# A five-step graph network on one Trainium2 core: where x and the output weights are transposed, and when adjacency pairs load

## The reference

```python
Af = A.astype(float32)                       # 2048 x 2048, symmetric, 0 or 1
state = x                                    # 2048 x 256
for _ in range(5):
    s_in  = state @ in_W.T + in_b
    s_out = state @ out_W.T + out_b
    a = concat([Af @ s_in, Af.T @ s_out, state])
    r = sigmoid(a @ r_W.T + r_b)
    z = sigmoid(a @ z_W.T + z_b)
    h = tanh(concat([Af @ s_in, Af.T @ s_out, r * state]) @ h_W.T + h_b)
    state = (1 - z) * state + z * h
out = tanh(state @ o1_W.T + o1_b) @ o2_W.T + o2_b
return layernorm(x + out)
```

## Time and profile before

| | |
|---|---|
| median of 3 runs | 664.06 us (664.0 to 664.29) |
| profiled execution | 664.53 us |
| its span, first to last instruction | 662.7 us |
| TensorE matmul busy | 650.3 us, 98%, 2940 instructions |
| VectorE busy | 516.4 us, 78% |
| ScalarE busy | 348.5 us, 53% |
| GpSimd busy | 51.9 us, 8% |
| mean granted TensorE clock | 0.995 of full speed |
| DMA | 46.72 MB, 90515 packets, 72176 of them under 512 bytes |

### The profile page before, as it was taken

How to read it: one execution, slowest core, us unless ns; L and a number is a source line. 1 busy time by engine, 2 the same in 40 slices (tenths; PEclk the granted TensorE clock), 3 DMA queues, 4 the chain that set the end, 5 groups by cost and what they waited for, 6 DMA issues and landing times.

```text
span 662.7 us, 8577 instructions
## 1 busy us (share of the span) xinstructions
PE 650.3 (98%) x2940; PEld 539.6 (81%) x2940; DVE 516.4 (78%) x838; ACT 348.5 (53%) x486; POOL 51.9 (8%) x49
## 2 busy tenths in 40 slices
PE   8999999999999999999999999999999999999993
PEld 7888888888888888888888888888888888888883
DVE  4976878699687969967796997687789858855886
ACT  2873735477156337724562683366057525724646
POOL 0074034200500000000000000000000000000002
PEclk9999999999999999999999999999999999999998
DMA  8996533213000130300003022000322200013003
GB/s 293 305 405 242 169 130 107 42 42 54 2 0 32 50 47 33 50 14 0 32 33 62 0 63 32 0 32 32 52 44 60 35 1 1 0 64 127 1 2 130
DMA packets 90515, 46.72 MB, mean 70 GB/s; under 512 B 72176, under 2 KB 78960, under 8 KB 90224
## 3 DMA queue, kind: packets, MB, share of 16 engines
q1 hardware_dynamic: 86128, 45.77, 23.9%
q10 hardware_dynamic: 4352, 0.53, 0.5%
HBM read 32.12 MB, written 11.53 MB: 66 GB/s over the span
## 4 chain that ended last, share of the span: by engine, by line
PE 93%; DVE 2%; SPq 2%; DMA 2%; ACT 1%; issue 0%; DVEq 0%
PE bank L561 26%; PE bank L548 17%; PE bank L550 17%; PE bank L549 17%; PE bank L612 15%; DMA stage<-in_adj_dram 2%; SPq L393 1%; DVE stats L1560 1%; DVE a L1553 0%; DVE ring L1136 0%; SPq L389 0%; ACT a L1120 0%; DVE work L1593 0%; SPq L391 0%; DVE work L1588 0%
## 5 line engine op out<-in xcount | busy, mean ns | idle before, releaser
L561 PE MATMUL bank<-ring,rows 128*128 128x512 f32 x768 | 178.8, 389 | 0.3 <-ACT stateT L1091 0.3
L561 PEld LDWEIGHTS bank<-ring,rows 128*128 128x128 f32 x768 | 144.0, 188 | 30.6 <-ACT stateT L1091 0.5
L901 ACT ACTIVATE work<-work,bias 128x512 f32<-128x512 f32 x120 | 86.2, 723 | 155.5 <-DVE work L1280 154.9
L1280 DVE SCALAR_TENSOR_TENSOR work<-degree,deg_w,bank 128x512 f32<-128x512 uint16 x120 | 88.7, 745 | 57.5 <-PE bank L550 56.5
L548 PE MATMUL bank<-u_c,fold 128*128 128x512 f32 x240 | 93.5, 389 | 0.0
L550 PE MATMUL bank<-u_c,fold 128*128 128x512 f32 x240 | 93.4, 389 | 0.0
L549 PE MATMUL bank<-u_c,fold 128*128 128x512 f32 x240 | 93.4, 389 | 0.0
L612 PE MATMUL bank<-ring,rows 128*128 128x512 f32 x256 | 65.1, 391 | 0.0
L548 PE MATMUL bank<-st_c,own 128*128 128x512 f32 x160 | 62.3, 389 | 0.0
L550 PE MATMUL bank<-st_c,own 128*128 128x512 f32 x160 | 62.2, 389 | 0.0
L549 PE MATMUL bank<-st_c,own 128*128 128x512 f32 x160 | 62.2, 389 | 0.0
(11 more groups left out here) (148 smaller groups left out, 985.0 us busy)
## 6 DMA issues: line engine op xcount, KB each, us to landing
stage<-in_adj_dram SPq DMA_DIRECT2D x15, 512.0 KB, 8.8
sums<-in_adj_dram SPq DMA_DIRECT2D x13, 512.0 KB, 8.5
turned_dram<-work SPq DMA_DIRECT2D x12, 512.0 KB, 2.6
rows<-turned_dram SPq DMA_DIRECT2D x192, 32.0 KB, 2.0
work<-in_x_dram SPq DMA_DIRECT2D x4, 512.0 KB, 10.2
x_dram<-work SPq DMA_DIRECT2D x4, 512.0 KB, 8.9
a<-x_dram SPq DMA_DIRECT2D x4, 512.0 KB, 5.3
a<-in_adj_dram SPq DMA_DIRECT2D x3, 512.0 KB, 11.5
```

The costliest lines, as they stand in the source:

```text
L561: m = nc.tensor.matmul(u_bank[2 * (c % 2) + d][:, :], rows[:, part, j, d * P:(d + 1) * P], tile[:, jj, :], start=(first and jj == 0 and pa ...
L901: nc.scalar.activation(gates[:, g, e, :], gates[:, g, e, :], ACT.Tanh if g == H else ACT.Sigmoid, bias=bias[:, g, e:e + 1]).then_inc(gate_ ...
L1280: nc.vector.scalar_tensor_tensor(out=gates[:, g, e, :], in0=degree[:, c * CW:(c + 1) * CW], scalar=deg_w[:, g, e:e + 1], in1=g_bank[s % 3] ...
```

## The change

- The output weights are no longer transposed on TensorE in the preparation. They are loaded as 32 x 32 squares that already lie in the place of their transpose (16 DMAs in runs of 128 bytes, `o_load`, issued ahead of pair 17). VectorE transposes the squares (`o_turn`), ScalarE and VectorE split them (`o_high`, `o_low`), all in gate chunk 0. `PREP` shrinks to 12 items.
- Chunk 0 of x is still transposed on TensorE, now ahead of the H fold. Chunks 1, 2 and 3 are loaded a second time as squares (8 DMAs each, `x_load`): chunk 1 ahead of pair 18, chunk 2 ahead of pair 26 and after chunk 1's are moved, chunk 3 after the last pair, into staging slot 0. VectorE transposes them straight into `stateT` (`x_turn`) at the places that `MOVED_AT` names.
- SyncE loads chunk k of x ahead of pair 2k, so two adjacency pairs load between the chunks. ScalarE and VectorE split x in the same rhythm.
- The store of the split output weights (`o_dram`) moves from before pair 9 to before pair 24. The first part of the degrees gets a place of its own in `t_flat` and no longer waits for that store.

```diff
@@ -140,7 +140,7 @@
         o_w = t_flat[:, 0:4 * DB * D].rearrange("p (a n k d) -> p a n k d", a=2, n=2, k=DB)
         t_rows = t_flat[:, :].rearrange("p (a n w) -> p a n w", a=2, n=3)
-        deg_part = t_flat[:, 0:CW]
+        deg_part = t_flat[:, 4 * DB * D:4 * DB * D + CW]
         res = sums[:, :, :, :].rearrange("p s k w -> p (s k w)").bitcast(F32).rearrange("p (c w) -> p c w", c=NC - 1)
...
@@ -151,7 +151,8 @@
         early = stateT[:, :, :].rearrange("p d n -> p (d n)")
         gate_raw = [g.rearrange("p (b k) -> p b k", b=DB) for g in (late[:, 0:NR], late[:, NR:2 * NR], res.rearrange("p c w -> p (c w)")[:, 0:NR])]
-        o_raw = late[:, 2 * NR:2 * NR + 2 * DB * D].rearrange("p (n b k) -> p n b k", n=2, b=DB)
+        o_squares = late[:, 2 * NR:2 * NR + 2 * DB * D].rearrange("p (n w) -> p n w", n=2)
+        o_T = late[:, 2 * NR - 2 * DB * D:2 * NR].rearrange("p (n w) -> p n w", n=2)
         gate_T = [g.rearrange("p (m d) -> p m d", d=D) for g in (early[:, 0:2 * DB * D], degree[:, :].bitcast(F32))]
         lin_raw = early[:, 2 * DB * D:4 * DB * D].rearrange("p (n b k) -> p n b k", n=2, b=DB)
...
@@ -183,6 +184,8 @@
+        x_spare = {1: stateT[:, :, 3 * CW:4 * CW], 2: stateT[:, :, 3 * CW:4 * CW], 3: staged[0].bitcast(F32)}
         PACK = 8
...
@@ -309,17 +317,16 @@
         std_ready = sem("f_std_ready")
-        N_PREP = NG * 4 + 2
+        N_PREP = NG * 4
         PREP = [(0, R), (1, R), ("fold", R), (0, Z), (1, Z), ("own", Z), ("own", R), (0, H), (1, H), ("own", H),
-                ("fold", Z), ("o", 0), ("o", 1), ("fold", H)]
-        SPLIT = [item for item in PREP if item[0] in ("own", "fold", "o")]
-        ACT_AHEAD = {("own", H): [("x", 0)], ("o", 1): [("x", 1), ("x", 2)],
-                     ("fold", H): [("turned", 0), ("pair", 0), ("turned", 1), ("pair", 1)]}
-        DVE_AHEAD = {("own", H): [("degree", R)], ("fold", Z): [("degree", Z)],
-                     ("o", 1): [("x", 0), ("degree", H)], ("fold", H): [("x", 1), ("x", 2)]}
+                ("fold", Z), ("fold", H)]
+        SPLIT = [item for item in PREP if item[0] in ("own", "fold")]
+        ACT_AHEAD = {("own", H): [("x", 0)],
+                     ("fold", Z): [("x", 1), ("pair", 0), ("pair", 1)], ("fold", H): [("turned", 0), ("turned", 1)]}
+        DVE_AHEAD = {("own", H): [("x", 0), ("degree", R)], ("fold", Z): [("degree", Z), ("x", 1), ("degree", H)]}
         def times_read(item):
...
@@ -385,25 +392,50 @@
             sp.dma_start(gate_raw[R][:, :, 2 * D:], r_v[:, :, 2 * D:]).then_inc(r_loaded[2], 16)
             sp.dma_start(gate_raw[H], h_W.rearrange("(b p) k -> p b k", p=P)).then_inc(w_loaded[1], 16)
-            for n, w in enumerate((o1_W, o2_W)):
-                sp.dma_start(o_raw[:, n], w.rearrange("(b p) k -> p b k", p=P)).then_inc(o_loaded, 16)
             for n, b in enumerate((in_b, out_b)):
                 sp.dma_start(lin_bb[:, n], b.partition_broadcast(P)).then_inc(io_b_loaded, 16)
-            for c in range(NC):
-                sp.dma_start(x_raw[:, c * BC:(c + 1) * BC, :], x_v[:, c * BC:(c + 1) * BC, :]).then_inc(x_loaded[c], 16)
+            def o_load():
+                for n, w in enumerate((o1_W, o2_W)):
+                    for q in range(NQ):
+                        for k in range(DB):
+                            sp.dma_start(o_squares[q * SQ:(q + 1) * SQ, n, k * D:(k + 1) * D].rearrange("a (i c) -> a i c", c=SQ),
+                                         w[:, k * P + q * SQ:k * P + (q + 1) * SQ].rearrange("(i a) c -> a i c", a=SQ)).then_inc(o_loaded, 16)
+            def x_load(c, spare):
+                for q in range(NQ):
+                    for e in range(DB):
+                        sp.dma_start(spare[q * SQ:(q + 1) * SQ, e, :].rearrange("a (i c) -> a i c", c=SQ),
+                                     x[c * CW:(c + 1) * CW, e * P + q * SQ:e * P + (q + 1) * SQ].rearrange("(i a) c -> a i c", a=SQ))\
+                          .then_inc(x_squares[c], 16)
             for c in range(NC):
                 for p in range(NP):
                     q = c * NP + p
+                    if q < NP and q % 2 == 0:
+                        k = q // 2
+                        sp.dma_start(x_raw[:, k * BC:(k + 1) * BC, :], x_v[:, k * BC:(k + 1) * BC, :]).then_inc(x_loaded[k], 16)
                     if (c, p) == (NC - 1, NP // 2):
                         turn_store(0, 0)
+                    if (c, p) == (2, 1):
+                        o_load()
+                    if (c, p) == (2, 2):
+                        sp.wait_ge(prep_read, times_read(("fold", H)))
+                        x_load(1, x_spare[1])
+                    if (c, p) == (NC - 1, 2):
+                        sp.wait_ge(x_moved, DB)
+                        x_load(2, x_spare[2])
                     slot, loads = slot_of(q)
                     if q == IN_RES:
                         sp.wait_ge(prep_read, times_read(("own", NG - 1)))
                         sp.dma_start(o2_bb, o2_b.partition_broadcast(P)).then_inc(o2_b_loaded, 16)
-                    if q == IN_RES + 2:
-                        sp.wait_ge(prep_read, times_read(("o", 1)))
+                    if (c, p) == (NC - 1, 0):
+                        sp.wait_ge(o_split, 2)
                         sp.dma_start(o_dram, t_flat[:, 0:4 * DB * D].bitcast(F32)).then_inc(o_stored, 16)
                     if 2 * NP <= q < 2 * NP + NC:
...
@@ -422,6 +454,9 @@
                     sp.dma_start(staged[slot], adj_v[:, 2 * p:2 * p + 2, c * CW:(c + 1) * CW]).then_inc(stage_loaded[slot], 16)
+            sp.wait_ge(pair_ready, last_in(0) + 1)
+            sp.wait_ge(pair_stored, last_in(0) + 1)
+            x_load(3, x_spare[3])
             turn_store(0, 1)
             for k in range(2):
...
@@ -508,7 +543,7 @@
             pool.wait_ge(o2_b_loaded, 16)
             pool.wait_ge(x_hi, NC)
-            pool.wait_ge(x_read, NC * DB)
+            pool.wait_ge(x_read, DB)
             pool.wait_ge(x_split, NC)
             for c in range(NC):
...
@@ -567,7 +602,9 @@
                 wait(pe, u_lo, (c - 1) * TWO)
-                pe.wait_ge(x_read, min(NC * DB, (c + 1) * TWO))
+                pe.wait_ge(prep_read, times_read(("own", Z)) if c == 0 else N_PREP)
+                if c == 1:
+                    pe.wait_ge(x_read, DB)
                 for p in range(NP):
                     pe.wait_ge(pair_ready, c * NP + p + 1)
...
@@ -628,7 +665,7 @@
                 if first:
                     if c == 0:
-                        pe.wait_ge(x_read, NC * DB)
+                        pe.wait_ge(prep_read, N_PREP)
                     if c < NC - 1:
                         degrees(c)
...
@@ -686,21 +723,20 @@
             def turn_x():
-                for c in range(NC):
-                    pe.wait_ge(x_loaded[c], 16)
-                    for d in range(DB):
-                        m = c * DB + d
-                        pe.wait_ge(prep_read, times_read(PREP[N_PREP + m - 8]))
-                        for b in range(BC):
-                            last = nc.tensor.transpose(bank[m][:, b * P:(b + 1) * P],
-                                                       x_raw[:, c * BC + b, d * P:(d + 1) * P], ident[:, :])
-                        last.then_inc(x_turned, 1)
+                pe.wait_ge(x_loaded[0], 16)
+                pe.wait_ge(prep_read, times_read((0, H)))
+                for d in range(DB):
+                    for b in range(BC):
+                        last = nc.tensor.transpose(bank[DB + d][:, b * P:(b + 1) * P], x_raw[:, b, d * P:(d + 1) * P], ident[:, :])
+                    last.then_inc(x_turned, 1)
             def prepare():
                 for n, (kind, g) in enumerate(PREP):
                     b_ = prep_bank(n)
+                    if (kind, g) == ("fold", H):
+                        turn_x()
                     if n >= 8:
                         pe.wait_ge(prep_read, times_read(PREP[n - 8]))
...
@@ -863,6 +896,8 @@
                 if not (isinstance(t, int) and t == 0):
                     act.wait_ge(state_new, (t - 1) * S_TWO + c * TWO + e + 1)
+                elif c > 0:
+                    act.wait_ge(x_moved, (c - 1) * DB + e + 1)
                 wait(act, gate_done, t * S_GATE + (c - 1) * GATE + 2 * DB)
                 high(st_c[:, HI, e, :], stateT[:, e, c * CW:(c + 1) * CW], st_hi)
...
@@ -921,6 +956,8 @@
                     if first and (c, s) == (NC - 2, 0):
                         degree_part(NC - 1)
+                    if first and c == 0 and s in (2, 3):
+                        o_high(s - 2)
                     if s < DB:
                         rs_high(t, c, s)
...
@@ -1050,10 +1089,9 @@
                     for p in range(DB, NP):
                         expand_staged(0, p)
-                        turned_x(p)
-                        if p == DB:
-                            x_high(NC - 1)
-                    act.wait_ge(x_read, NC * DB)
+                        if p % 2 == 0 and p < NP - 2:
```

(27 more changed lines are left out.)

27 lines of the change are left out of this document (15 added, 12 removed).

## The result

| | before | after |
|---|---|---|
| median | 664.17 us (664.0 to 664.99) | 678.81 us (677.92 to 680.61) |
| ratio, 95% interval | | 1.0223 (1.0211 to 1.0234) |
| profiled execution, its span | 664.53, 662.7 us | 678.04, 676.2 us |
| mean granted clock | 0.995 | 0.985 |

The change makes the kernel 2.2% slower. 669.8 us was predicted, with 674.0 as the upper end. The direction was right. The loss from before's median, 14.6 us, is more than twice the 5.7 us forecast.

A forecast was written before the change was run, and what follows sets the result against it. TensorE's nearly unbroken stream was taken as the first bound, DMA second, VectorE third. Terms -3.7 + 0.8 + 0.1 + 2.9 + 5.6 = +5.7 us, added to the median 664.06, gave 669.8 us, range 666.0 to 674.0.

The forecast's parts named there:

- Part 1: Start: TensorE loses 32 small matmuls and pair 0 is ready in time, so aggregation starts near 21.7, -3.7 us.
- Part 2: Adjacency pairs between x chunks: pair 7 lands about 34.1, cast by 35.2, wanted at 34.4, +0.8 us (0 to 2).
- Part 3: Gate chunk 0: added VectorE work of about 3.8 us eats slack, +0.1 us (0 to 0.5); full time if VectorE is late.
- Part 4: Chunk 0: 24 loads on SyncE's queue ahead of the last residual store delay VectorE's first product, +2.9 us (0 to 5).
- Part 5: Before gate chunk 3: x chunk 3's eight loads ahead of the row loads delay T2, +5.6 us (4.5 to 7.5).
- rival C: Before chunk 3: as the main forecast, and TensorE's clock falls in the 5.6 us gap; chance 0.20.
- B: Chunk 0: the residual store lands in time and pairs are not delayed, +2.8 us, 666.9 us; chance 0.20.
- D: At T2: row loads barely late, the 5.6 us vanish; without the residual wait too, -2.8 us, 661.3 us; chance 0.09.
- E: x's 128-byte runs drain at half the row loads' pace; Part 4 and Part 5 each grow about 3 us, 676 us; chance 0.06.

The follow-up runs named there:

- e7_x_first: Kernel with both edits (24 loads behind the residual store, x chunk 3 on ScalarE's queue), plus all four x chunks loaded ahead of pair 0: 662.04 us.
- e3_both: Changed kernel with the 24 loads behind the last residual store and x chunk 3's loads on ScalarE's queue: 661.04 us, ratio 0.9958.
- e6_x1_late: Changed kernel with only x chunk 1's eight loads moved behind the last residual store; the output weights' 16 stay ahead of pair 17: 673.12 us.
- e1_late: Changed kernel with the 16 output-weight loads and 8 of x chunk 1 moved behind the last residual store and pair 19: 667.20 us.
- e5_wide: Changed kernel with the same 24 loads at the same places, as whole rows (768 runs, not 8,192), so values not transposed: 673.11 us.
- e8_fill0: Changed kernel with 28 matmuls on constants filling TensorE's first wait of 6.3 us in chunk 0: 679.94 us.
- e4_fill: Changed kernel with 18 matmuls, their result unread, filling TensorE's wait before gate chunk 3 in step 0: 677.21 us.
- e2_x3_on_act: Changed kernel with x chunk 3's eight loads issued on ScalarE's queue at the start of gate chunk 2: 672.87 us.

## Why the prediction was right and wrong

**Part 1 (-3.7) was right.** -3.50 at the first aggregation matmul, -3.70 at the gates of chunk 0. e7_x_first, which loads x ahead of the pairs, gains 2.7 us up to the same gates, and the pairs give 1.2 us more in e3_both. The forecast put the 3.7 down to matmuls and to pair 0 being ready in time, without splitting it.

**Part 2 (+0.8 for pair 7) did not come.** The stream of 128 matmuls has no gap in it, 29.28 us against 29.48. Pair 7 came in time: ScalarE, after a wait of 1.77 us for it, started its cast at 32.99, where the forecast had it land at 34.1, and was done at 34.05, before TensorE wanted it at 21.87 + 7 x 1.81 = 34.5. ScalarE waited 0.24 to 0.28 us for each of the next five pairs.

**Part 3 (+0.1) was right for a kernel without other lateness.** In e3_both VectorE's added work costs nothing. Its other sentence, that it costs its full time if VectorE is late, holds too: from the product to the degree cast VectorE was busy 21.42 of 25.38 us before, and 24.73 of 25.01 after. The idle 3.96 us in which it could have caught up are filled. 10.03 us late at the product, less 0.37, gives the 9.66 us. It also says why half clock costs nothing in after's profile: VectorE ran almost without a gap, and the clock was back (1.00 from 72 us) before the matmuls that do not wait for it (from 72.99). In the five other profiles with a late product it was 0.50 during part of them, for 1.6 to 2.8 us lost. No part of the forecast has a fall of the clock in chunk 0.

**Part 4 (+2.9) had the right mechanism and is the mis-sized term: with part 3 it measured +9.7.** The store was to land at 60.8 and landed at 67.0. Two terms of that step, the issue time of the loads and the landing time of the store, failed.
- *The issue: 56.2 predicted, 59.62 measured.* I took 0.50 us a load from the earlier trace rows, where little else moves. Here the 24 loads took 17.5 us rather than 12. Within the 16 loads of the weights the time of one differs:

```profile
44.45 3.59 SPq L403 DMA_DIRECT2D a<-in_L_gnn_o_W_dram  x3
```

```profile
47.59 3.90 SPq L403 DMA_DIRECT2D a<-in_L_gnn_o_W_dram  x8
```

```profile
39.50:48.00 8.50, 8.50 (x39) 7.06 (x38) 7.85 (x14) 6.55 (x9) 7.19 (x6) 1.00 0.97 278
48.00:51.50 3.50, 3.50 (x17) 2.88 (x17) 0.09 (x1) 0.00 (x0) 3.34 (x3) 1.00 0.45 69
```

  The first excerpt is of 45 to 48 us, three loads in 3.59 us; over the first eight (39.63 to 47.59) it is 1.00 us each, while the DMA engines are at 0.97. The last eight, in the second excerpt, take 0.49 us, and now the engines are at 0.45, for a load of 32 KB gives them less than 0.49 us of work. I read this as a group that is held back by full engines first and then leaves them idle: (1 - 0.45) x 3.5 = 1.9 us of a resource that my engines' figure counted as always full.
- *The landing: 4.6 us predicted (60.8 - 56.2), 7.4 measured.* I had the figure for a loaded queue in the earlier trace rows, 10.3 us, and reasoned from 2.6 for a store alone. Behind the store SyncE issues three pairs within 3.2 us, and 62 to 67 us runs at a DMA share of 0.96. e6_x1_late shows the same landing at another time, and in e1_late and e3_both, with the store ahead of the loads, it took 10.2 and 11.3 us and was in time all the same. How much of it is work queued ahead of the store and how much the pairs behind it was not separated.
- The rest: the product was wanted at 57.1 and not 57.9, as part 2 did not come, +0.8.

My rows give 3.4 us of the engines for 4,096 small runs, and 407 GB/s where large ones are loaded: 6.8 us for the 8,192 against 2.6 for the same 1 MB in large runs, so 4.2 us for the small runs, an estimate. After against e5_wide shows 5.3 us at the store's landing. The measurement decides.

**Part 5 (+5.6) had the right mechanism; it measured 7.4, in two terms that were both off.** The wait is 4.3 us, below the low end. SyncE's order was as forecast: eight issues in 4.04 us, and the row loads start at 121.30, which less the 6.18 us of earlier shift is 6.3 later than in the earlier trace rows (6.1 forecast). T2 came at 139.05, which less the same 6.18 is 132.87, 4.9 later than in the earlier trace rows and not 6.1: before it started 3.0 us after SyncE had issued its last row load, now 1.65 us. I had carried the 3.0 over. TensorE's slack of 0.5 behind it measured 0.7. The other term is the clock, 3.0 us, which stood as rival C with a chance of 0.20. The rows for it were in hand: at the end of the trace of before the last matmul ended at 652.7 and the clock left 1.00 in 656.0 to 656.5, under 4 us later, and a gap of 5.6 us was forecast. A forecast that has a gap longer than such a fall took should have put the fall into the sum. How long the clock stays low after work resumes no row of before shows; in after it was 0.50 from 144 to 150 us.

**The account.** Predicted +5.7, measured +13.5 in the span. Of the 7.8 us between them part 2 is -0.8, parts 3 and 4 +6.7, part 5 -1.3 for the wait and +3.0 for the clock, and 0.2 remain in small shifts. The medians lie another 1.1 us apart; of that no profile was taken. Half clock on the 18 matmuls, as in the five other profiles, would give such a loss in after's slower runs, but this is not shown.

**The rivals.** B (the store lands in time) was far off. D, the faster one, was wrong for after, but its price of -2.8 us is what e3_both does: 661.04 against 664.14, -3.1. E, runs at half pace, gave 676 us, nearest to the result: e5_wide shows the small runs to be half of the product's lateness in chunk 0 (whether as half the pace was not measured), while in chunk 3 the eight loads took 0.50 us each and gave no such delay, so E's number is near by luck. The range was too narrow because two of the DMA figures behind part 4 (0.50 us an issue and 2.6 us a landing) came from stretches with little else to move, the third (60.3) took the engines as always full, and the clock stood in no bound of it.

## What to carry to other kernels

SyncE issued its DMAs in the order of the program, so a new group of small loads cost all that stood behind it: with the 24 loads ahead of it the residual store left at 59.62 us, with them behind it at 43.22 (e1_late), and with the eight ahead of them the row loads started at 121.30, 6.3 us later than in the earlier trace rows beyond the 6.18 us of earlier shift. Read the queue from that point on, find the one transfer that an engine without slack waits for, and place the group behind it or on an idle queue. Here that turned 2.2% slower into 0.4% faster with the same work (e3_both). Price an issue and a landing by rows from an equally loaded stretch. If the forecast contains TensorE waits of several microseconds, put half clock into the sum (in after the clock fell to 0.50 in the waits of 6.27 and 4.28 us), and ask which matmuls it will fall on: the six that wait for VectorE anyway in after's chunk 0 lost nothing, the 14 at the start of chunk 3 lost 3.0 us.

## What the runs showed of the hardware beyond what was expected

- A 32 KB load in 128-byte runs took SyncE 0.49 us where the DMA engines were at 0.45, and 1.00 us where they were at 0.97. In e1_late 16 of them took 14.31 us, 0.89 each.
- A 512 KB store landed after 7.4 us behind those loads, after 10.2 and 11.3 us ahead of them (e1_late, e3_both), and after 2.6 us where little else was moved.
- In after the clock fell 3.6 us after the end of TensorE's last matmul ahead of chunk 3 and 2.7 us in chunk 0, to 0.50, and in e5_wide 1.9 us after it. In e6_x1_late (68.3) and e8_fill0 (75.6) it fell just after TensorE had resumed from a wait of 2.8 us, with a shorter wait a few microseconds earlier. In after it stayed at 0.50 to 150 us, 6 us after TensorE was working without a gap again. Matmuls on data that nothing reads held it at 1.00 (e4_fill, 140 to 150 us; e8_fill0, 62 to 75 us).
- The time of chunk 0 differed from 40.7 to 44.0 us between profiled executions of kernels with the same queue ahead of the store (after, e2_x3_on_act, e4_fill, e8_fill0), along with the landing of that store and with half clock on the 18 matmuls (none in after, 1.6 to 2.0 us in the others). The runs of e2_x3_on_act and e6_x1_late lie up to 6 us apart, those of e3_both 1.5. Why the landing varies was not settled.
